# The second half of the third LayerNorm's transposed rows through the bank of q, and the rounding of y1 behind k and v

## The reference

```
x = layernorm(x + windowed_attention(x))       # 16 heads of 64, windows of 128
x = layernorm(x + int8_linear(x))              # x quantized by one scale over all of x
x = layernorm(x + gelu(linear_attention(x)))   # q, k, v of 1024 columns each
x = layernorm(x + mlp(x))                      # 256 -> 1024, relu squared, -> 256, plus a low rank term
```

## Time and profile before

| what | value |
|---|---|
| median of 3 runs | 3224.38 us (3223.12 to 3226.81) |
| the profiled execution's own time | 3225.97 us |
| its span, first to last instruction | 3224.1 us |
| mean granted TensorE clock | 0.986 |
| TensorE busy | 3016.3 us (94%) |
| VectorE busy | 2384.7 us (74%) |
| ScalarE busy | 2164.9 us (67%) |
| GpSimd busy | 1649.6 us (51%) |

### The profile page before, as it was taken

How to read it: one execution, slowest core, us unless ns; L and a number is a source line. 1 busy time by engine, 2 the same in 40 slices (tenths; PEclk the granted TensorE clock), 3 DMA queues, 4 the chain that set the end, 5 groups by cost and what they waited for, 6 DMA issues and landing times. The chain is left out here.

```text
span 3224.1 us, 70305 instructions
## 1 busy us (share of the span) xinstructions
PE 3016.3 (94%) x21167; PEld 2498.1 (77%) x21167; DVE 2384.7 (74%) x6865; ACT 2164.9 (67%) x5664; POOL 1649.6 (51%) x2222
## 2 busy tenths in 40 slices
PE   5999999999999999999999997799999999999986
PEld 4888788778778778778778785577888888888875
DVE  5877877877867867867867875687777777777764
ACT  4766666755755755756756764577788888778774
POOL 3655545645644644645645654344555554555455
PEclk9999999999999999999999999799999999999998
DMA  2000000000000000000000001200000000000000
GB/s 80 8 15 18 12 15 15 16 15 15 15 15 15 15 16 15 15 16 15 15 16 8 15 21 40 66 14 7 14 14 14 21 21 14 14 14 14 8 14 20
DMA packets 50150, 58.70 MB, mean 18 GB/s; under 512 B 2848, under 2 KB 47920, under 8 KB 49472
## 3 DMA queue, kind: packets, MB, share of 16 engines
q1 hardware_dynamic: 47056, 51.78, 5.1%
q10 hardware_dynamic: 2672, 1.87, 0.2%
HBM read 36.86 MB, written 16.78 MB: 17 GB/s over the span
## 5 line engine op out<-in xcount | busy, mean ns | idle before, releaser
L577 POOL TENSOR_SCALAR a_ex<-a_ex,a_rc 128x384 f32<-128x384 f32 (+1 forms) x1024 | 531.2, 532 | 753.9 <-DVE a_rc L489 753.5
L386 ACT ACTIVATE a_ex<-a_sm,a_nm 128x384 f32<-128x384 f32 (+1 forms) x1024 | 572.4, 560 | 100.8 <-DVE a_nm L482 97.8
L482 DVE CUSTOM_DVE_ANT_0 a_sm<-sc,a_mask,a_rn 128x384 f32<-128x384 f32 (+1 forms) x1024 | 531.6, 544 | 46.4 <-PE sc L267 44.2
L392 ACT ACTIVATE a_pt<-tp 128x256 f32<-128x256 f32 (+1 forms) x512 | 219.8, 429 | 306.1 <-PE tp L278 306.1
L1525 POOL TENSOR_TENSOR b_alo<-b_ring,b_ahi 128x512 fp32r<-128x512 f32 x128 | 169.2, 1322 | 469.7 <-DVE b_ring L1390 403.2
L236 PE MATMUL pj<-a_whi,a_xhi 128*128 128x384 f32 x1024 | 397.7, 388 | 2.5 <-DVE a_rb L460 2.5
L561 POOL TENSOR_TENSOR a_qr<-a_ra,a_rb 128x256 f32<-128x256 f32 x512 | 367.0, 731 | 36.8 <-DVE a_rb L460 36.6
L267 PE MATMUL sc<-a_kT,a_qT 64*128 64x384 f32 (+1 forms) x2048 | 346.4, 457 | 2.4 <-DVE a_nm L482 1.0
L236 PE MATMUL pj<-a_whi,a_xlo 128*128 128x384 f32 x1024 | 346.7, 339 | 0.0
L236 PE MATMUL pj<-a_wlo,a_xhi 128*128 128x384 f32 x1024 | 345.6, 337 | 0.0
L288 PE MATMUL qk<-a_pt,a_v 128*64 128x128 f32 x5120 | 314.6, 278 | 32.2 <-issue 21.8
(11 more groups left out here) (202 smaller groups left out, 8033.9 us busy)
## 6 DMA issues: line engine op xcount, KB each, us to landing
a_xin<-x SPq DMA_DIRECT2D x16, 512.0 KB, 3.9
a_xres<-x SPq DMA_DIRECT2D x16, 512.0 KB, 3.9
y<-a_res SPq DMA_DIRECT2D x16, 512.0 KB, 3.1
b_y<-y SPq DMA_DIRECT2D x16, 512.0 KB, 3.8
out<-b_y SPq DMA_DIRECT2D x16, 512.0 KB, 2.9
a_xin<-wqkv SPq DMA_DIRECT2D x8, 256.0 KB, 2.8
a_pt<-wqkv SPq DMA_DIRECT2D x1, 1536.0 KB, 6.9
a_ot<-wqkv SPq DMA_DIRECT2D x1, 1536.0 KB, 10.6
```

The costliest lines, as they stand in the source:

```text
L386: e.activation(ex[h][w][:, 0:width], sm[h][w % 2][:, 0:width], ACT.Exp, bias=nm[:, w, h:h + 1], scale=-1.0, accum_out=rs[:, w, h:h + 1]).t ...
L392: e.activation(pt[0][w][:, 0:width], TP[:, 0:width], ACT.Copy).then_inc(g['pt_act'], 1)
L482: e.tensor_tensor_reduce(out=sm[h][w % 2][:, 0:width], in0=SC[w % 2][h][:, 0:width], in1=mem['mask'][:, off:off + width], scale=rn[:, par, ...
L577: e.tensor_scalar(row, row, 0.0, rc[:, w, h:h + 1], ALU.add, ALU.mult).then_inc(g['exn_pool'], 1)
```

## The change

The second half of y3 goes through Q_BANK. The transpose into it waits until VectorE has read the last chunk of q of the unit in hand; the next unit's first q waits until the second y3lo is done. The first halves stay in T, and the waits for T ask for the first y3lo alone. The round of y1 stands behind k's and v's reads in VectorE's step 7.

```diff
         if c == 0:
             e.wait_ge(n2.sems['y_act'], s + 1)
             if due(s - 2):
-                e.wait_ge(g['y3l_dve'], 2 * (s - 2))
+                e.wait_ge(g['y3l_dve'], 2 * (s - 2) - 1)
...
+    def y3_bank(c):
+        return Q_BANK if c else T
+
     def pe_y3(e, s, c):
         if c:
-            e.wait_ge(g['y3l_dve'], 2 * s + 1)
+            if inside(s + 1):
+                e.wait_ge(g['qu_dve'], HC * (s + 1) + HC)
+            else:
+                e.wait_ge(g['y3l_dve'], 2 * s)
         else:
             e.wait_ge(n3.sems['y_act'], s + 1)
             if inside(s + 3):
...
             else:
-                e.wait_ge(g['y3l_dve'], 2 * s)
-        pe_rows_transpose(e, T, y3_rows(s), c, ident[:, :]).then_inc(g['y3_pe'], 1)
+                e.wait_ge(g['y3l_dve'], 2 * s - 1)
+        pe_rows_transpose(e, y3_bank(c), y3_rows(s), c, ident[:, :]).then_inc(g['y3_pe'], 1)
...
         if due(HC * s + c):
             e.wait_ge(g['qu_dve'], HC * s + c)
+        if c == 0 and due(s - 1):
+            e.wait_ge(g['y3l_dve'], 2 * (s - 1))
         pe_chunk(e, 'q', Q_BANK, s, c).then_inc(g['q_pe'], 1)
...
-    def act_high(e, pe, out, dst, s, c):
+    def act_high(e, pe, out, bank, dst, s, c):
         e.wait_ge(g[pe], 2 * s + c + 1)
-        e.activation(dst[:, c, :], T[:, :], ACT.Copy).then_inc(g[out], 1)
+        e.activation(dst[:, c, :], bank[:, :], ACT.Copy).then_inc(g[out], 1)
...
-    def dve_low(e, act, out, dst, hi, s, c):
+    def dve_low(e, act, out, bank, dst, hi, s, c):
         e.wait_ge(g[act], 2 * s + c + 1)
-        e.tensor_tensor(dst[:, c, :], T[:, :], hi[:, c, :].bitcast(F32), ALU.subtract).then_inc(g[out], 1)
+        e.tensor_tensor(dst[:, c, :], bank[:, :], hi[:, c, :].bitcast(F32), ALU.subtract).then_inc(g[out], 1)
...
-        if c == 7 and inside(b + 3):
-            dve_round(e, b + 3)
         if inside(kv[0]):
             dve_k(e, *kv)
             dve_v(e, *kv)
+        if c == 7 and inside(b + 3):
+            dve_round(e, b + 3)
```

More of the change, by code:

```diff
@@ L1298, in act_step @@
         if c == 0 and inside(b - 2):
-            act_high(e, 'y3_pe', 'y3h_act', mem['y3hi'], b - 2, 1)
+            act_high(e, 'y3_pe', 'y3h_act', y3_bank(1), mem['y3hi'], b - 2, 1)
         if c == 1 and inside(b + 2):
@@ L1308, in act_step @@
         if c == 0 and inside(b + 1):
-            act_high(e, 'y2_pe', 'y2h_act', mem['y2hi'][(b + 1) % 2], b + 1, 0)
+            act_high(e, 'y2_pe', 'y2h_act', T, mem['y2hi'][(b + 1) % 2], b + 1, 0)
         if inside(b):
@@ L1312, in act_step @@
         if c == 0 and inside(b + 1):
-            act_high(e, 'y2_pe', 'y2h_act', mem['y2hi'][(b + 1) % 2], b + 1, 1)
+            act_high(e, 'y2_pe', 'y2h_act', T, mem['y2hi'][(b + 1) % 2], b + 1, 1)
         if c == 2 and inside(b - 1):
@@ L1327, in act_step @@
         if c == 7 and inside(b - 1):
-            act_high(e, 'y3_pe', 'y3h_act', mem['y3hi'], b - 1, 0)
+            act_high(e, 'y3_pe', 'y3h_act', y3_bank(0), mem['y3hi'], b - 1, 0)
         act_weights(e, b, c)
@@ L1444, in dve_step @@
         if c == 0 and inside(b - 2):
-            dve_low(e, 'y3h_act', 'y3l_dve', mem['y3lo'], mem['y3hi'], b - 2, 1)
+            dve_low(e, 'y3h_act', 'y3l_dve', y3_bank(1), mem['y3lo'], mem['y3hi'], b - 2, 1)
         if c == 1 and inside(b - 3):
@@ L1466, in dve_step @@
         if c == 0 and inside(b + 1):
-            dve_low(e, 'y2h_act', 'y2l_dve', mem['y2lo'][(b + 1) % 2], mem['y2hi'][(b + 1) % 2], b + 1, 0)
+            dve_low(e, 'y2h_act', 'y2l_dve', T, mem['y2lo'][(b + 1) % 2], mem['y2hi'][(b + 1) % 2], b + 1, 0)
         if c == 3 and inside(b - 1):
@@ L1479, in dve_step @@
         if c == 0 and inside(b + 1):
-            dve_low(e, 'y2h_act', 'y2l_dve', mem['y2lo'][(b + 1) % 2], mem['y2hi'][(b + 1) % 2], b + 1, 1)
+            dve_low(e, 'y2h_act', 'y2l_dve', T, mem['y2lo'][(b + 1) % 2], mem['y2hi'][(b + 1) % 2], b + 1, 1)
         if inside(at[0]):
@@ L1485, in dve_step @@
         if c == 7 and inside(b - 1):
-            dve_low(e, 'y3h_act', 'y3l_dve', mem['y3lo'], mem['y3hi'], b - 1, 0)
+            dve_low(e, 'y3h_act', 'y3l_dve', y3_bank(0), mem['y3lo'], mem['y3hi'], b - 1, 0)
         dve_weights(e, b, c)
```

## The result

| | before | changed |
|---|---|---|
| median, beside each other | 3227.85 us (6 runs) | 3202.39 us (6 runs, 3198.20 to 3204.43) |
| ratio | | 0.9922, interval 0.9909 to 0.9935 |
| profiled execution | 3225.97 us | 3201.29 us |
| its span | 3224.10 us | 3199.50 us |
| TensorE busy | 3016.3 us | 3010.4 us |

Faster by 0.8%. Beside later experiments the same changed kernel came out at 3203.46 against 3226.17 (ratio 0.9928) and 3205.28 against 3226.84 (0.9935), so 22 to 25 us less in three measurements; 22.7 had been worked out. In the changed kernel all lines named here except 1073 and 1079 move by 8: k's read is 1365, v's 1372, the round 1344 and 1346, q's 1403 and 1407, square 1415, y3lo and y2lo 1359, rhi 1287, the ones to y3hi and y2hi 1232, alo 1533, rlo 1541, the bias 1502.

What follows compares the result with a forecast made beforehand. TensorE was taken as the bound. Eleven boundaries at 1.46 us (16.1) plus 3.1, 1.3, 1.7 and 0.5 at the ends made 22.7 us, so 3202 us was predicted, range 3197 to 3216.

Steps and rivals of the forecast that it cites:

- The bound and the pause: Layers: TensorE bounds, idling 1.49 us per period before y3's second-half transpose, 27.3 us in 16 pauses over the layers.
- The bank of q: At b = 5 the second y3 transpose no longer waits; q's new wait for the second y3lo has 0.54 us of room.
- The round: Behind k and v on VectorE, with GpSimd idle, y1's round takes 0.75 + 0.69 us, not 0.99 + 1.67.
- The delay of q's read: VectorE's line 1395 before the change starts 0.20 us later because y1's round now stands ahead of it.
- The boundary: Between units, b = 2 to 12: transpose 1.71 us earlier, 0.25 given back at y2, 1.46 gained, eleven times.
- b = 13 and 14: Boundaries without a round: about 1.6 us each, the second partly bound by chains, 3.1 us together.
- b = 15 and 16: Last units: 1.7 us at the first, where up waits for the second y3lo, and 0.5 at the last.
- At b = 1: First boundary: second y3 transpose waits for q's read, 1.3 us gained of the 4.02 us pause, 2.7 remain.
- The slow stretch behind the pause: After b = 1's pause products last 0.63 us, not 0.4; a possible 1.4 us gain was kept for the range.
- The second (2.66 us in the new place): Rival, chance 0.12: y1's round stays 2.66 us long, q's read is 1.37 later, gain 8.7 us, time 3215.7.
- The third (the gain given back at v): Rival, chance 0.08: up's wait for v grows by the boundary's gain; only the end gains, some 4 us, 3220.
- The fourth: Rival, chance 0.04: TensorE's new wait before q for the second y3lo makes the kernel slower, 3235 us.

Runs made afterwards that it cites:

- y3_late: Changed kernel with ScalarE's second y3hi behind k's two activations in step 0; 3215.79 us against 3228.13 for the kernel before, ratio 0.9961.
- bank_only: Kernel before with only y3's second half moved to q's bank, y1's round left ahead of k and v; 3206.27 us against 3226.17, ratio 0.9935.
- round_late: Changed kernel with y1's round moved behind ahi and at, beside GpSimd's alo; 3228.68 us against 3226.17 for the kernel before, ratio 1.0007.
- round_only: Kernel before with only y1's round moved behind k and v, both y3 halves still through T; 3228.71 us against 3226.17, ratio 1.0005.
- bank_again: Second measurement of the kernel before with only the bank moved; 3205.75 us against 3226.84 for the kernel before, ratio 0.9931.
- sums_late: Changed kernel with VectorE's small sums behind the first y2lo instead of ahead of it; 3202.73 us against 3228.13 for the kernel before, ratio 0.9919.
- k_first: Changed kernel with ScalarE's two k activations ahead of the third LayerNorm in step 7; 3203.44 us against 3228.13 for the kernel before, ratio 0.9923.
- again: The changed kernel itself, unaltered, measured a second time; 3203.46 us against 3226.17 for the kernel before, ratio 0.9928.

## Why the prediction was right

**The bound and the pause.** Right. The busy time of TensorE in ten periods is the same (673 us), and the 1.49 us of pause are gone, less what y2 gives back. Forecast 22.7 us; the profiles show 22.1 behind the start-up, the medians 22 to 25.

**The bank of q.** Right: no wait for q's read in the periodic part, q's own new wait with 0.63 us of room (0.54 worked out). That this wait is real, and how far it was from costing time, y3_late shows.

**The round.** The choice between 1.44 and 2.66 us was right, and carried the forecast: all twelve rounds from b = 1 on took 0.75 + 0.69. VectorE's busy time fell by 13.4 us over the kernel, near the 14.6 of twelve times 1.22; bank_only shows that this is not where the gain comes from. The prediction put the old 0.99 + 1.67 down to rlo alone; the first line stood beside alo, as the rows under round_late show, which changes nothing in the choice. The description of the kernel before calls the round due nine steps later; it is two (step 7 to step 1 of the next b), and in the changed kernel at b = 5 ScalarE turns it to bf16 at 2466.55, 12.4 us behind its end. The delay of q's read was mis-sized, 0.1 us instead of 0.20: the first line starts with the read of v's accumulator (2452.66) and not 0.04 us behind it. The Trainium skill (SBUF — State Buffer, "Who interferes with whom") has GpSimd and a VectorE tensor_scalar in a two-port mode exclude each other, with whoever starts first holding on; the trace agrees in both orders (1.72 for alo, 1.66 for the round in round_late, against 1.31 and 0.69).

**The boundary.** 1.46 worked out, 1.39 measured. The term that was missing is kb. In the kernel before, the bias on GpSimd ended at 2468.71, 1.4 us before kb:

```profile
2470.12 0.11 DVE L1371 TENSOR_TENSOR b_kb<-b_su,b_bv 128x8 f32<-128x8 f32 x1
...
2466.31 2.40 POOL L1494 TENSOR_TENSOR b_y<-b_y,b_bias 128x1024 f32<-128x1024 f32 x1
```

The work behind the boundary moved up, and the bias, which hangs behind alo and rlo, did not move up with it. In the changed kernel kb starts at 2460.85 under the running bias and ends at 2461.20, 0.04 us behind the bias's end at 2461.16. That is 0.24 us on the chain to y2lo, against the 0.1 us by which the round's delay came out smaller: so the second y2 transpose is 0.28 us late where 0.15 was worked out. Behind it up starts 0.06 us later than after no pause, where 0.10 had been set aside for issue and refill; together 0.34 instead of 0.25. The Trainium skill (SBUF — State Buffer, "Who interferes with whom") says that a VectorE instruction with two inputs in SBUF excludes a GpSimd instruction that reads there: kb is one (su and bv), and the trace agrees.

**The parts at the ends.** b = 13 and 14 brought 3.4 (3.1 worked out), b = 15 and 16 with the rest 2.4 (2.2). At b = 1 it was 1.0 instead of 1.3, with 3.0 us of pause instead of 2.7. q's read was not the reason: it was 0.1 us late there too. TensorE came to the first transpose some 0.4 us sooner (5.76 us behind the start of ScalarE's third LayerNorm instead of 6.15), because GpSimd's alo no longer began under the round's first line (before, out's products started 0.05 us behind alo's end; now alo ends before they are due):

```profile
2178.02 1.74 POOL L1525 TENSOR_TENSOR b_alo<-b_ring,b_ahi 128x512 fp32r<-128x512 f32 x1 [2.14 <-DVE b_ring L1390]
```

```profile
2175.92 1.30 POOL L1533 TENSOR_TENSOR b_alo<-b_ring,b_ahi 128x512 fp32r<-128x512 f32 x1 [2.14 <-DVE b_ring L1398]
```

(The first row is of the kernel before, the second of the changed one.) The runs agree: the pause is 4.52 us in round_only against 4.02 before, and 2.52 in bank_only and bank_again against 3.02 in the changed kernel. That makes 0.5 us more of pause for the move, 0.4 from TensorE being sooner and 0.1 from q's read being later, where 0.2 was worked out: the 0.3 us that b = 1 is short. The 0.4 us are not lost, they stand in the row of the start-up. The slow stretch behind the pause stayed, as assumed: 4.84 us to the first y2 transpose, at a granted clock of 0.65. But it comes and goes with the execution and not with the change: in bank_only, sums_late and k_first the same work took 3.3 us at a granted clock of 1.00, and in bank_again, the code of bank_only with the same pause, 4.8 us at 0.64. At b = 15 the time was right and the reason not: not up waits for y3lo, but out for alo, for 1.6 us instead of the few tenths that I had set aside; so only 1.4 us of waiting for y3lo were left, where the prediction had about 4.

**The rivals.** The second (2.66 us in the new place) is ruled out by the rows of the round, and round_late shows what it would have taken. The third (the gain given back at v) by the wait at v, 0.6 us as before; k_first shows its true half: ScalarE's and VectorE's chain through step 7 is right behind TensorE, and taking that wait away brings nothing. The fourth by the room of 0.63 us in front of q; y3_late shows that even 1.63 us more would not have made the change a loss.

**Is the round's move needed?** No run shows a use for it. Bank_only has the shorter period by 0.08 us, and bank_again the same median as the changed kernel beside it. Over eleven boundaries the move costs about 1 us (an estimate from the periods), which the medians cannot tell.

## What to carry to other kernels

When a pause of the bounding engine is about one buffer with two users in a row, look for a bank that has just been read and isn't wanted for some microseconds; check the wait that it puts in front of the bank's owner by working the chain through with the new times. Before an instruction is moved, look at what it shared its old place with: its duration in the profile belongs to that company, and it can halve or double in the next place (0.99 + 1.67 us for the round here became 0.75 + 0.69, and 0.75 + 1.66 four instructions on). After such a gain look again at small instructions that used to stand clear of another engine's long one.

## What the runs showed of the hardware

- The round's second instruction (128x1024 float32, two scalar operations) took 0.69 us with GpSimd idle and 1.66 us with a GpSimd tensor_tensor begun ahead of it, ending 0.56 us behind that; the other way round GpSimd's alo took 1.72 instead of 1.31.
- A VectorE tensor_tensor of 128x8 took 0.35 us instead of 0.12 under GpSimd's bias, ending 0.04 us behind it. So even an eight-column instruction took three times as long when it came at the wrong moment; in four kernels it showed 0.35 to 0.37 when under the bias and 0.12 in the five others looked at.
- Behind the pause of TensorE at b = 1 the same 16 products and transposes took 3.3 us at a granted clock of 1.00 (2.4 GHz) in three executions (bank_only, sums_late, k_first) and 4.8 to 4.9 us at 0.64 to 0.65 in four others (before, after, again, bank_again). The length of the pause did not decide it: 2.52 us in both bank_only (1.00) and bank_again (0.64).
